# Routing and row transfers moved beside attention, and sorting for both eight-expert stages

## The reference

```
L0: cross attention to ctx (8x64 keys), 16 heads of 8, mask;  then causal self attention and 4 mixed experts, top 2
L1: cross attention, 16 heads of 64, masked;                  then 8 experts, F = 512, top 2 of softmax
L2: cross attention, 16 heads of 8, no mask;                  then 8 experts, F = 256, top 2 of the logits
L3: two-way attention;                                        then 64 experts of 64, top 6 in 4 of 8 groups
```

```
out = out + (silu(x @ w1[i]) * (x @ w3[i])) @ w2[i] * w[i]
```

## Time and profile before

| stretch of the span, us | stage | length |
|---|---|---|
| 32 to 131 | first small attention | 99.0 |
| 206 to 392 | self attention | 186.0 |
| 541 to 669.6 | wide attention | 128.6 |
| 669.6 to 754.4 | normalisation, choice, scatters, first load | 84.8 |
| 754.4 to 887.6 | sorted experts, row returns | 133.2 |
| 912 to 998.8 | second small attention | 86.8 |
| 998.8 to 1020 | normalisation, splits | 21.2 |
| 1020 to 1169.7 | gated experts | 149.7 |
| 1260 to 1591 | last experts | 331.0 |

### The profile page before, as it was taken

One profiled execution on the slowest core, in us unless ns is written; L12 is line 12 of the kernel. 1 busy time (PEld: TensorE's weight loads), 2 busy tenths in 40 slices (PEclk: granted clock), 3 DMA queues, 4 the chain that ended last, 5 costly groups with the idle time before them and its releaser, 6 DMA issues. The chain is left out here.

```text
span 1596.8 us, 24399 instructions
## 1 busy us (share of the span) xinstructions
PE 1283.8 (80%) x7148; PEld 1032.2 (65%) x7148; DVE 1024.7 (64%) x2047; ACT 734.5 (46%) x1260; POOL 620.8 (39%) x598
## 2 busy tenths in 40 slices
PE   4896669997997899721997499699946659999997
PEld 2673459987664599720886267588833438787875
DVE  3885678887324276660665466677768767667675
ACT  2443446665332554430654254455523325455553
POOL 1311634431000133245233131389844116676665
PEclk9996779999898899955999599699976669999998
DMA  3500011110000000131111100133202025343333
GB/s 89 143 0 1 0 41 36 39 39 5 1 0 0 20 1 0 60 112 55 35 48 32 44 1 0 45 97 97 95 19 103 1 60 125 109 130 115 126 115 104
DMA packets 69931, 85.64 MB, mean 54 GB/s; under 512 B 14282, under 2 KB 40269, under 8 KB 69850
## 3 DMA queue, kind: packets, MB, share of 16 engines
q1 hardware_dynamic: 67250, 79.94, 17.3%
q0 software_dynamic: 2272, 4.24, 0.8%
q10 hardware_dynamic: 336, 0.59, 0.2%
HBM read 69.98 MB, written 8.92 MB: 49 GB/s over the span
## 5 line engine op out<-in xcount | busy, mean ns | idle before, releaser
L2356 POOL TENSOR_TENSOR e_h<-e_h,e_gate 128x512 f32<-128x512 f32 x128 | 187.8, 1484 | 145.8 <-DVE e_h L2408 89.9
L2413 DVE TENSOR_TENSOR e_h_low<-e_h,e_h_high 128x512 fp32r<-128x512 f32 x132 | 117.8, 893 | 75.6 <-ACT e_h_high L2343 75.4
L2343 ACT ACTIVATE e_h_high<-e_h 128x512 fp32r<-128x512 f32 x132 | 83.5, 633 | 97.8 <-POOL e_h L2356 90.1
L228 PE MATMUL n_ps_t<-ident,n_zn 128*128 128x128 f32 x128 | 34.4, 433 | 90.5 <-DVE n_zn L167 82.7
L2408 DVE TENSOR_TENSOR e_h<-e_s,e_ps_b 128x512 f32<-128x512 f32 x132 | 89.4, 678 | 13.1 <-ACT e_s L2328 8.7
L1001 PE MATMUL u_ps_o<-u_vaug,u_pT 128*128 128x72 f32 x768 | 96.9, 269 | 0.0
L1001 PEld LDWEIGHTS u_ps_o<-u_vaug,u_pT 128*128 128x128 f32 x768 | 93.3, 192 | 0.0
L2328 ACT ACTIVATE e_s<-e_ps_a 128x512 f32<-128x512 f32 x132 | 77.7, 589 | 31.5 <-PE e_ps_a L1364 28.4
L228 PEld LDWEIGHTS n_ps_t<-ident,n_zn 128*128 128x128 f32 x128 | 23.9, 224 | 98.2 <-DVE n_zn L167 78.3
L932 POOL TENSOR_TENSOR u_kbd<-u_keys,groupmask 96x512 fp32r<-96x512 f32 x60 | 62.8, 1067 | 62.4 <-DMA u_keys<-s_k 37.2
L1028 ACT ACTIVATE u_sm<-u_sm 128x512 f32<-128x512 f32 x96 | 60.6, 631 | 54.5 <-DVE u_sm L1060 53.9
(11 more groups left out here) (439 smaller groups left out, 3901.3 us busy)
## 6 DMA issues: line engine op xcount, KB each, us to landing
e_gate<-gates_by_expert SPq DMA_DIRECT2D x256, 128.0 KB, 3.0
e_gate<-gates_by_expert SPq DMA_DIRECT2D x32, 256.0 KB, 3.4
w_raw<-in_L1w SPq DMA_DIRECT2D x24, 256.0 KB, 4.2
u_qs<-s_q SPq DMA_DIRECT2D x16, 192.0 KB, 2.6
u_keys<-s_k SPq DMA_DIRECT2D x8, 384.0 KB, 3.5
w_w<-in_L2w SPq DMA_DIRECT2D x24, 128.0 KB, 2.7
sorted<-blank SPq DMA_DIRECT2D x1, 2535.0 KB, 17.6
e_zb<-sorted SPq DMA_DIRECT2D x13, 195.0 KB, 2.5
```

The costliest lines, as they stand in the source:

```text
L2343: nc.scalar.activation(h_parts[k % 3][0][:, :], h[k % 3][:, :], ACT.Copy).then_inc(high_ready, 1)
L2356: nc.gpsimd.tensor_tensor(h[c % 3][:, :], h[c % 3][:, :], gate[pair % SLOTS][:, :], ALU.mult)\
L2413: nc.vector.tensor_tensor(h_parts[k % 3][1][:, :], h[k % 3][:, :], h_parts[k % 3][0][:, :], ALU.subtract).then_inc(low_ready, 1)
```

## The change

1. `rotate` writes all steps out; `live` is a plain comparison. In both attentions, in all three places, `ps_t` is one bank: transposes go in two halves of four, each half between the halves of the scores, and ACT copies each half by itself.
2. A new class `Router` has a piece of program for each engine, called in every step of the wide attention (first eight-expert stage) and of the second small attention (second stage). For a group of four tiles it does, in successive steps: statistics and variance, reciprocal root (Ln and Exp on ACT), normal rows, turn, logits, pick of two (`max`, `max_index`), ranks and places, and two row scatters per step from step 12. Eight steps follow the 16 tiles instead of four; the last group's 8 scatters stand at the start of `experts_sorted`.
3. Places no longer depend on the counts of other experts: each expert has a fixed region of 2048 rows (and 128 to spare), 17280 rows in all, in two buffers, both filled with blank rows (two DMAs of 9.0 MB in place of one of 2.5). A table with the first row of every block is made at the end (`block_table`).
4. `experts_sorted` serves both stages. SP loads each block by itself from a row read from the table: three register reads and three DMAs per batch; six batch buffers in the second stage, three in the first. The weights' raw buffers are loaded during attention (4 experts, 8 in the second stage); silu writes into h.
5. Gone: two normalisations, `StreamedExperts`, `experts_gated`. The wide attention's weights are loaded during the normalisation before it, with a wait. `then_load` now stands behind the load of y.

```diff
-def rotate(eng, step, lags=LAGS):
+def rotate(step, lags=LAGS):
-    for t in range(4):
-        step(t, t, t // TPB)
-    with eng.Fori(1, TILES // 4) as i:
...
+    for t in range(TILES + lags):
+        step(t, t % 4, t // TPB)
...
+class Router:
+    def dve(self, dve, t):
+        if 4 <= t < TILES + 4:
+            dve.drain()
+            nc.vector.bn_stats(self.stats[:, t - 4, :], self.x[:, t - 4, :])
+        if t % 4 == 3 and 7 <= t < TILES + 4:
+            self.variance(dve, (t - 7) // 4)
+        if t % 4 == 0 and 8 <= t < TILES + 8:
+            self.normal_rows(dve, (t - 8) // 4)
+        if t % 4 == 2 and 10 <= t < TILES + 8:
+            self.pick(dve, (t - 10) // 4)
+        if t % 4 == 3 and 11 <= t < TILES + 8:
+            self.places(dve, (t - 11) // 4)
+        if t == TILES + 7:
+            self.block_table(dve)
...
+    def normal_rows(self, dve, g):
+        dve.wait_ge(self.root_ready, g + 1)
...
+    def pick(self, dve, g):
+        dve.wait_ge(self.logits_done, g + 1)
...
+    def places(self, dve, g):
+        dve.wait_ge(self.ranked, g + 1)
...
+    def pe(self, pe, t):
+        if t % 4 == 1 and 9 <= t < TILES + 8:
+            pe.wait_ge(self.normed, g + 1)
...
+            for j in range(GROUP):
+                last = nc.tensor.transpose(self.ps[:, j * P:(j + 1) * P], self.rows[0][:, g * GROUP + j, 0:D], self.ident)
...
+        if t % 4 == 2 and 10 <= t < TILES + 8:
+            pe.wait_ge(self.z_out, g + 1)
+            for j in range(GROUP):
+                last = nc.tensor.matmul(self.ps[:, j * E:(j + 1) * E], self.zT[:, tile * P:(tile + 1) * P],
...
+        if t % 4 == 3 and 11 <= t < TILES + 8:
+            pe.wait_ge(self.picks_ready, g + 1)
+            nc.tensor.matmul(self.ps[:, 2 * n:3 * n], self.sort["ones"], cells, start=True, stop=True)
...
+    def pool(self, pool, t):
+        if t < 12:
+            return
+        if t == 12:
+            pool.wait_ge(self.prefilled, 16 * 2)
...
+        for k in range(PICKS):
+            self.nc.gpsimd.indirect_dma_start(
...
# attend_small, PE
-                    for h in range(2):
+                for h in range(2):
+                    if live(t, 0):
                         last = nc.tensor.matmul(ps_s[p][:, h * 512:(h + 1) * 512], qs[p][:, :],
...
-                    pe.wait_ge(p_ready, t)
-                    wait(pe, pT_ready, t - 1)
-                    for j in range(8):
...
+                    if live(t, 1):
+                        if h == 0:
+                            pe.wait_ge(p_ready, t)
+                        wait(pe, pT_ready, 2 * (t - 1) + h)
+                        for j in range(4):
...
# attend_small, DVE, ahead of mask and maximum
+                if router is not None:
+                    router.dve(dve, t)
...
# experts_sorted, SP
+            sp.wait_ge(router.table_ready, 1)
             sp.wait_ge(scattered, 16 * PICKS * TILES)
             for q in range(BATCHES):
                 if q >= NZ:
                     for j in range((q - NZ) * BATCH, (q - NZ + 1) * BATCH):
                         sp.wait_ge(*stored(j))
-                src = sorted_dram[q * BATCH * P:(q + 1) * BATCH * P, :].rearrange("(b p) c -> p b c", p=P)
-                sp.dma_start(zb[q % NZ][:, :, :], src).then_inc(zb_loaded[q % NZ], 16)
+                for i in range(BATCH):
+                    j = q * BATCH + i
+                    row = sp.value_load(router.table[0:1, 1, j:j + 1], min_val=0, max_val=SORTED_ROWS - P)
+                    sp.dma_start(zb[q % NZ][:, i, :], sorted_dram[bass.ds(row, P), :]).then_inc(zb_loaded[q % NZ], 16)
...
-                    nc.scalar.activation(s[j % 2][:, :], gate_side[j % 2], ACT.Silu).then_inc(s_ready, 1)
+                    nc.scalar.activation(h[j % 2][:, :], gate_side[j % 2], ACT.Silu).then_inc(s_ready, 1)
...
-                                 blank[:, :].unsqueeze(1).broadcast_to([P, BLOCKS, ROW])).then_inc(prefilled, 16)
+                                 blank[:, :].unsqueeze(1).broadcast_to([P, SORTED_ROWS // P, ROW])).then_inc(prefilled, 16)
```

More of the change, by code:

```diff
@@ L452, in _ @@
             last.then_inc(zeroed, 1)
+            if router is not None:
+                router.first_dve(dve)
             def step(t, r, b):
@@ L561, in _ @@
             last.then_inc(zeroed, 1)
+            if router is not None:
+                router.first_pool(pool)
             def step(t, r, b):
@@ L697, in step @@
                     nc.vector.tensor_tensor(row, row, ps_o[:, 0:D], ALU.add).then_inc(x_done, 1)
-            rotate(dve, step)
+                if router is not None:
+                    router.dve(dve, t)
+            rotate(step, LAGS + extra)
 HG = 4
@@ L1870, in _ @@
                 if j < BLOCKS:
[L1871 removed]
+                    offs[j] = nc.tensor.value_load(router.table[0:1, 0, j:j + 1], min_val=0, max_val=(E - 1) * weights.span)
                     up(j, offs[j])
@@ L1977, in _ @@
-            nc.vector.tensor_reduce(expert[:, :], passed[:, :, :], X, ALU.add)
-            dve.drain()
-            nc.vector.tensor_scalar(table[:, :], expert[:, :], float(E - 1), float(weights.span), ALU.min, ALU.mult)\
-                .then_inc(table_ready, 1)
             for e in range(E):
@@ L2619, in build @@
             experts_mixed(nc, "e0_", x, x2, self_w, zT, logits[4], rank)
+        early.close()
         clear_spent(nc)
-        normalise(nc, "n4_", x, idn, root_ln, zT, then=ACT.Exp)
-        with ExitStack() as stack:
-            ml = Memory(nc, stack, "a1_")
-            kT_all, vT_all = ml.sb("kT", [P, 8, B * KEYS]), ml.sb("vT", [P, 8, B * KEYS])
-            project_wide(nc, "p1_", wide1, ctxT, kT_all, vT_all)
-            attend_wide(nc, "t1_", x, wide1, zT, kT_all, vT_all, idn, neg1, ident_b[:, :],
-                        loads=load(later, later_loaded))
@@ new lines, in build, with loads @@
+            router.span = weights.span
+            with ExitStack() as inner:
+                ml = Memory(nc, inner, "a1_")
+                wide1 = {n: ml.sb("L1" + n, sh) for n, sh in (
+                    ("wq", [P, 1024]), ("wk", [P, 1024]), ("wv", [P, 1024]), ("wo", [P, 8, D]), ("bq", [P, 8]),
+                    ("bk", [P, 8]), ("bv", [P, 8]), ("bo", [P, D]))}
+                wide_loaded = ml.sem("wide_loaded")
+                normalise(nc, "n4_", x, idn, root_ln, zT, then=ACT.Exp,
+                          loads=load([(t, A["L1" + k]) for k, t in wide1.items()], wide_loaded))
+                kT_all, vT_all = ml.sb("kT", [P, 8, B * KEYS]), ml.sb("vT", [P, 8, B * KEYS])
+                arrive(nc, wide_loaded, 16 * len(wide1))
+                project_wide(nc, "p1_", wide1, ctxT, kT_all, vT_all)
+                def loads(sp):
+                    load(later, later_loaded)(sp)
+                    weights.first_loads(sp)
+                attend_wide(nc, "t1_", x, wide1, zT, kT_all, vT_all, idn, neg1, ident_b[:, :], loads=loads, router=router)
```

740 lines of the change are left out of this document (309 added, 431 removed).

## The result

The changed kernel takes 1643.52 us, the median of five runs (1638.59 to 1656.01), against 1601.03 for the kernel before (five runs, 1595.55 to 1608.32). The ratio is 1.0296, 95% interval 1.025 to 1.0342: slower by 42.5 us. The forecast was 1628, 25 us slower than the median shown then, with a range to 1658; the direction was right and the size too small.

What follows compares the result with a forecast made beforehand. PE was taken to bound the attention and expert stages, with winnable gaps between. Terms +23+.5-24+24+31-34+5 = +25.5 on the profiled 1598.7 us gave 1624, 1628 on the median's basis; range 1580 to 1658.

Steps and rivals of the forecast that it cites:

- Step 1: First small attention: half the transposes and half the scores join the softmax chain, 6.48 us per tile; +23 us.
- the price by bytes: Blank fill, two times 9.0 MB: landing time scaled by bytes, 125 us; costed at 0, up to 29 us if others are caught.
- Step 2: Wide attention to first sorted block: router work among tiles added, but the gap behind the attention shortened; -24 us.
- The fourth group's chain: Behind the wide attention's last x: the last router group's steps with nothing beside them, through the table; 17.5 us.
- Step 3: First sorted experts stage: three register reads and loads per batch make rows late, 2.4 us per batch; +24 us.
- Step 4: Second small attention: changed PE order +8, router steps ahead of the tile's maximum and scatters the remainder; +31 us.
- the chain of 5.16 us: Second small attention: softmax chain per tile with half the transposes and half the scores added, against 4.55; +8 us.
- Step 5: Second experts stage: sorted blocks at 1.85 us replace normalisation, splits and gated experts; -34 us.
- Step 6: Clock: new stalls in the first sorted stage and second small attention pull stretches to the low level; +5 us.
- Rival B: First sorted stage: row loads land inside the slack, so the kernel gets faster, 1585 us; chance 0.27.
- C: Whole kernel near no change: loads cost half and router waits fall in Exp's shadow, 1606 us; chance 0.18.
- D: Whole kernel much slower: DVE locks scatters, blank fill blocks SP, or 2.3 us a block; about 1665 us; chance 0.08.

Runs made afterwards that it cites:

- experiment 5: Kernel before with only the changed attentions (one bank, interleaved halves) and the unrolled loop, no router, old routing: 1646.16 us, ratio 1.0295.
- experiment 9: Changed kernel mended (attention order, row-load waits), sorting first stage only: 1578.43 us; PE's router step last in wide attention: 1569.46; both stages sorted, router last: 1571.32.
- Experiment 6: Kernel before, but DVE makes the weights' low parts only after all 32 row scatters have landed: 1599.89 us in one run.
- experiment 7: Kernel before with two extra indirect DMAs, whose rows point nowhere, on POOL ahead of the 32 row scatters: 1595.46 us in one run.
- Experiment 2: Changed kernel, but SP waits before each block's load only for the store of the block that used its place: 1624.76 us, ratio 1.0168.
- experiment 3: Changed kernel, but SP reads a batch's three row numbers before it waits for the stores: 1631.75 us, ratio 1.0204.
- experiment 4: Changed kernel, but in the second small attention DVE does the router's step behind the tile's maximum and subtraction: 1630.84 us, ratio 1.0193.
- experiment 1: Changed kernel, but in both small attentions PE issues the whole scores before the transposes, still halves in one bank: 1631.85 us, ratio 1.0205.

## Why the forecast was right in direction and too small

**Step 1 (+23): right.** 22.7 by the stage, and the chain as worked out: transposes' half and scores' half behind Exp, 6.48 us, where twelve of fifteen steps are 6.5. By the pitch it is 25.8; the first Exp comes 4 us sooner. That the single bank holds PE for .74 us a tile by itself wasn't in the sum, and in this order it does no harm, since the second half of the scores hides it. Two banks and whole scores together bring it back to 4.95. The unrolled loop is harmless by the same measurement. So is the blank fill: the second of two 8.8 MB landed 93.0 us after issue (125 by the price by bytes), and experiment 5, with the old fill of 2.5 MB, is as long up to the self projection (167.6).

**Step 2 (-24): -18.** Two terms were off and in part cancel. Among the tiles 24.1 were added and not 15: 3.9 are the halves, which I had put at nothing there, and 20.2 the router. Of these, 8.2 are PE's step standing ahead at the end, with the clock that fell (experiment 9); that clock I had placed in the two other stages. The other 12 are not divided between DVE's work and the rest; I had exposed two fifths of DVE's 25.2 us (10.1, where the sum has 9.9) and 4.8 of PE's. The fourth group's chain took 18.8 us from last x to table (17.5). The scatters took 12.4 us, not the 18.4 that I took from the earlier trace rows. By the Trainium skill's rule (SBUF — State Buffer, "two separate sides") the second operation waits for one instruction of the other. The changed kernel agrees, with 1.61 us beside low parts of 1.22, and so do all ten profiles with the router (longest 1.93). Three profiles without it don't: 6.60, 6.61 and 6.97 beside four experts' low parts, in the kernel before and experiments 5 and 7. Experiment 6 (one profile) shows that those low parts are the cause, experiment 7 that a first use is not. Why the same row of low parts lets the scatters through in the changed kernel stays open.

**Step 3 (+24): right,** 25.4. Experiment 2 takes it all back, experiment 3 divides it in reads (18) and loads (7).

**Step 4 (+31): too small, and the term that made the error.** 43.1. The mechanism was the right one; three of its sizes were not. The halves alone make 12.7 there (I had 8): the chain of 5.16 us is seen as 5.2, but the first two steps take 6.5 where they took 3.2 and 3.4. The router on top makes 30.4 (I had 23). Tile 12 is 10.1 us over the 5.2, where I had 3.6 for DVE's step and 1.9 for the two scatters: I priced the scatters' own time and not POOL's wait for DVE's places, which keeps the queries from PE (experiment 4). The seven other tiles from 8 on are 21.6 over it, where I had 17.4. Moving DVE's step takes 19 us away (experiment 4). The split between halves and router holds for taking them in this order: with the router there, undoing the scores' order gives nothing back (experiment 1).

**Step 5 (-34): -26.5.** Blocks at 2.00 us, within 1.47 to 2.3, taken as 1.85: 6 us of the difference. The first block needs 6.7 us from its first product (1125.4) to its output (1132.1), which a count of 39 pitches leaves out but for one: 5 more. From last Exp to table 32.6 and not 28. Scatters and loads to the first block 20.4 and not 27.7, as no scatter was held long (the longest 1.38).

**Step 6 (+5).** The loss is there, in more places: .83 in the second small attention, .74 in the last 26 us of the wide one (experiment 9). Its share isn't separated from the waits that caused it. The self attention's late clock is an accident of two of the profiles.

Rival B (faster, by loads inside the slack) is ruled out by ten waits in ten batches. C and D did not come: the loads cost their full price, and neither fill nor lock did harm. What would have told more beforehand is to price the halves apart from the router: the earlier trace rows gave 31 of their 39 us, and 39 is nearly the whole slowdown of 42.5.

## What to carry to other kernels

When work is laid beside a stage, look at what the stage gives up to make room: here the half bank and the interleaving, taken alone, cost 39 us, and the rest of the change nothing net until it was mended. Put the added step behind the instruction that the chain waits for, and look for it on every engine: on DVE that won 19 us in the small attention and on PE 8 in the wide one; on POOL it cured a step of 15.5 us, but others grew. Where a load is divided into parts, divide its wait too: the parts that could go early then hide the last.

## What the runs showed of the hardware

A read of a table value into SP's register costs .6 us (experiment 3). One scatter can be held for four experts' low parts, 6.6 to 7.0 us: so in the three profiles without the router in which low parts stand beside the scatters, and in none of the ten with it (longest 1.93). With PE busy the whole time the granted clock stayed at .50 for 14 us in two of the profiles and was 1.00 there in another execution of the same kernel; the stage took 186.6 and 186.7 us in these two and 177.3 to 177.6 in the twelve others.
